# Silu as one ScalarE operation between two table loads, in the delta-rule stage of a three-layer kernel

## What is computed

```
q = silu(_short_conv(x @ Wq.T, conv_q))        # the same for k and v, four taps
beta = jax.nn.sigmoid(x @ Wb.T)
q, k = _l2norm(q), _l2norm(k)                  # per head
def step(S, inp):                              # a scan over the 512 tokens
    q_t, k_t, v_t, b_t = inp
    v_new = (v_t - einsum('bhd,bhdm->bhm', k_t, S)) * b_t[..., None]
    S = S + einsum('bhd,bhm->bhdm', k_t, v_new)
    return S, einsum('bhd,bhdm->bhm', q_t, S)
```

## Time and profile before

| | |
|---|---|
| median of 3 runs | 744.13 us (742.5 to 744.98) |
| profiled execution | 742.86 us, its span 741.1 us |
| granted TensorE clock, mean | 0.936 of full speed |
| busy: PE, DVE, ACT, POOL | 610.2, 596.0, 477.6, 471.5 us |
| steps begin on DVE at (us) | 52.4, 90.1, 134.5, 180.8, 227.2, 273.6, 319.6, 362.8 |

### The profile page before, as it was taken

The page is one execution under the profiler, slowest core; times in us unless marked ns, Lnnn a source line. Parts: engine busy times, 40 slices in busy tenths (PEclk is TensorE's granted clock), DMA queues, the critical chain, the costliest instruction groups (busy, mean ns, idle before and its releaser), DMA issues.

```text
span 741.1 us, 17464 instructions
## 1 busy us (share of the span) xinstructions
PE 610.2 (82%) x5443; PEld 490.8 (66%) x5443; DVE 596.0 (80%) x1698; ACT 477.6 (64%) x1270; POOL 471.5 (64%) x494
## 2 busy tenths in 40 slices
PE   4826365897998979977687989989999999979797
PEld 3614143685876858766567658768887787957776
DVE  4499989899999999999988768888897888654435
ACT  3984748799797996967367647465574736563442
POOL 2017999699898998989928714425507723673534
PEclk9956666899999999999998989999999999999999
DMA  6331221303214031130020343345546645655722
GB/s 233 74 76 57 57 75 47 100 16 83 65 42 118 14 74 57 40 105 15 1 71 2 100 111 116 101 145 154 154 134 173 179 128 148 187 165 142 201 86 75
DMA packets 104687, 72.70 MB, mean 98 GB/s; under 512 B 44832, under 2 KB 92576, under 8 KB 104352
## 3 DMA queue, kind: packets, MB, share of 16 engines
q1 hardware_dynamic: 100000, 62.27, 29.6%
q0 software_dynamic: 4608, 9.45, 4.7%
HBM read 44.48 MB, written 27.20 MB: 97 GB/s over the span
## 4 chain that ended last, share of the span: by engine, by line
PE 25%; ACT 7%; DVE 6%; SPq 4%; issue 4%; DMA 4%; POOL 1%; DVEq 0%; ACTq 0%; POOLq 0%
PE bank L2146 4%; PE bank L2127 4%; PE bank L2050 3%; PE bank L2019 3%; PE bank L2174 2%; PE bank L1882 2%; ACT prod_mem L1321 2%; PE bank L2117 1%; DMA hid<-in_w 1%; ACT wv L1363 1%; SPq L637 1%; POOL s_xs L966 1%; PE bank L2056 1%; SPq L640 1%; PE bank L1854 1%
## 5 line engine op out<-in xcount | busy, mean ns | idle before, releaser
L1854 PE MATMUL bank<-w,hid 128*128 128x128 f32 x768 | 100.5, 287 | 24.5 <-DVE y_even L2737 13.1
L1854 PEld LDWEIGHTS bank<-w,hid 128*128 128x128 f32 x768 | 95.5, 201 | 34.6 <-ACT hid L1189 10.8
L898 POOL TENSOR_TENSOR oq_mem<-hist_mem,q_t 128x384 f32<-128x384 f32 (+1 forms) x96 | 101.4, 1090 | 0.0
L1189 ACT ACTIVATE hid<-bank 128x512 f32<-128x512 f32 x112 | 62.4, 594 | 35.6 <-PE bank L1834 34.9
L2146 PE MATMUL bank<-w,wv 128*128 x428 | 61.1, 286 | 11.6 <-ACT wv L1363 10.9
L2146 PEld LDWEIGHTS bank<-w,wv 128*128 128x128 f32 x428 | 53.0, 194 | 18.5 <-issue 18.1
L2605 DVE TENSOR_REDUCE hist_mem<-hist_mem 128x64 f32<-128x320 f32 x128 | 62.3, 486 | 3.4
L981 POOL DMA_INDIRECT qkv<-s_ys,back_at x32 | 30.4, 952 | 52.5 <-DMA s_ys<-q_t 42.6
L1762 PE MATMUL bank<-xnT_h,wtap_h 128*128 128x512 f32 x104 | 49.7, 478 | 16.1 <-DVE qkv L2559 6.7
L1832 PE MATMUL bank<-xT_h,w_h 128*128 128x512 f32 x112 | 50.7, 453 | 11.7 <-ACT hid L1189 11.5
L2595 DVE TENSOR_REDUCE u<-prod_mem 128x32 f32<-128x288 f32 x128 | 57.6, 450 | 3.4
(11 more groups left out here) (302 smaller groups left out, 1745.4 us busy)
## 6 DMA issues: line engine op xcount, KB each, us to landing
hid<-in_w SPq DMA_DIRECT2D x72, 128.0 KB
s_qkv<-qkv SPq DMA_DIRECT2D x24, 256.0 KB, 2.6
pin<-s_xs SPq DMA_DIRECT2D x71, 64.0 KB
pin<-s_qkv SPq DMA_DIRECT2D x16, 256.0 KB, 2.9
kk<-in_w SPq DMA_DIRECT2D x30, 128.0 KB
s_ys<-q_p SPq DMA_DIRECT2D x28, 128.0 KB
s_ys<-q_t SPq DMA_DIRECT2D x23, 128.0 KB
s_xs<-zeros SPq DMA_DIRECT2D x40, 64.0 KB
```

The source lines that it names most:

```text
L898: tt(oq[:, :, j, :, 0:HD], s_at, bc(turned[:, n, j], 2, HD), ALU.mult).then_inc(o_part, 1)
L1189: nc.scalar.activation(hid[:, e % 2, f], bank[:, ZB + f, :], ACT.Relu).then_inc(hid_ready, 1)
L1854: last = nc.tensor.matmul(bank[:, y_bank(e, wide), tokens], hid[:, e % 2, f, tokens], w2[:, e, f], start=(f == 0), stop=(f == FC - 1))
```

## The change

ACT now applies Silu itself, from the bank into qkv, one operation for each of q, k and v; the three sigmoid operations and DVE's multiplication are gone. Silu is in another table set than Exp and Ln, so a load stands before and one behind each group: two in each of the steps 0 to 5 and six in the opening. `out_norm` (Ln, Exp) moves ahead of the first load, v's Silu and the second load ahead of `xf_rstd`. PE projects v ahead of `moe_down(n, 3)`, still behind `out_project`. `delta_kdot` on DVE moves from gap (5, 0) to (4, 2). In the opening, SP stores k of chunk 0 before it loads chunk 2's x, and loads it back before v.

```diff
             v_out(0, first=True)
             beta_out(0)
+            k_out(0)
             first_x(2)
+            beta_in(0)
+            k_in(0)
             v_in(0)
-            beta_in(0)
-            k_out(0)
-            k_in(0)
             q_out(0)
...
-            def prep_sigmoid(c, z):
-                src = bank[:, (QB, KB, QB)[z], :]
+            def prep_silu(c, z):
                 act.wait_ge(projected, 4 * c + z + 1)
-                nc.scalar.activation(sig[:, z], src, ACT.Exp, scale=-1.0).then_inc(sig_exp, 1)
-                act.wait_ge(sig_exp, 3 * c + z + 1)
-                nc.scalar.activation(sig[:, z], sig[:, z], ACT.Ln, bias=one_col[:]).then_inc(sig_log, 1)
-                act.wait_ge(sig_log, 3 * c + z + 1)
-                nc.scalar.activation(sig[:, z], sig[:, z], ACT.Exp, scale=-1.0).then_inc(sig_ready, 1)
+                if due(16 * c):
+                    act.wait_ge((q_stored, k_stored, v_stored)[z], 16 * c)
+                nc.scalar.activation(qkv[:, z], bank[:, (QB, KB, QB)[z], :], ACT.Silu).then_inc(silu_ready, 1)
...
                 if out:
                     out_square(o)
-                if prep:
-                    prep_sigmoid(c, 0)
-                if out:
                     out_norm(o)
                 if prep:
-                    prep_sigmoid(c, 1)
+                    nc.scalar.preload_act_table_set("silu_and_others")
+                    prep_silu(c, 0)
+                    prep_silu(c, 1)
                 delta_turn(i)
                 if out:
                     xf_centre(o)
                 if moe:
                     moe_scale(n, 3, wide=False)
                     moe_expert(n, 4)
+                if prep:
+                    prep_silu(c, 2)
+                    nc.scalar.preload_act_table_set("natural_log_exp_and_others")
                 if out:
                     xf_rstd(o)
                 if moe:
                     moe_expert(n, 5)
                 if out:
                     xf_scale(o)
-                if prep:
-                    prep_sigmoid(c, 2)
...
             w1_round()
-            first_sigmoid(0, 2)
-            first_sigmoid(1, 0)
+            nc.scalar.preload_act_table_set("silu_and_others")
+            first_silu(0, 2)
             first_square(0, 0)
+            first_silu(1, 0)
+            nc.scalar.preload_act_table_set("natural_log_exp_and_others")
             xn_centre(2)
             first_norm(0, 0)
-            first_sigmoid(1, 1)
-            first_sigmoid(1, 2)
+            nc.scalar.preload_act_table_set("silu_and_others")
+            first_silu(1, 1)
+            first_silu(1, 2)
             first_square(1, 0)
             first_square(1, 1)
+            nc.scalar.preload_act_table_set("natural_log_exp_and_others")
             first_beta(1)
...
                 if out:
                     out_project(o)
+                if prep:
+                    prep_project(c, 2)
                 if moe:
                     moe_down(n, 3, wide=False)
                     moe_up(n, 4)
-                if prep:
-                    prep_project(c, 2)
-                if moe:
                     moe_up(n, 5)
...
-                elif at == (5, 0):
+                elif at == (4, 2):
                     if ahead:
                         delta_kdot(i + 1)
...
-                elif at == (6, 3):
-                    if prep:
-                        prep_silu(c, 0)
```

More of the change, by code:

```diff
@@ L1383, in taps_round, with first_silu @@
                 nc.scalar.copy(wtap_h[:, TAPS[g]], wtap[:, TAPS[g]]).then_inc(taps_high, 1)
-            def first_sigmoid(c, r):
+            def first_silu(c, r):
                 z, name = ((1, "k"), (2, "v"), (0, "q"))[r]
@@ L1389, in first_sigmoid @@
                 if c:
[L1390 to L1395, removed]
+                    act.wait_ge((k_stored, v_stored, q_stored)[r], 16)
+                nc.scalar.activation(qkv[:, z], bank[:, FIRST_BANKS[c][name], :], ACT.Silu).then_inc(silu_ready, 1)
             def first_beta(c):
@@ L1433, in _ @@
             first_rstd(1)
+            nc.scalar.preload_act_table_set("silu_and_others")
             taps_round(1)
             taps_round(2)
-            first_sigmoid(0, 0)
-            first_sigmoid(0, 1)
+            first_silu(0, 0)
             first_square(0, 1)
+            first_silu(0, 1)
+            nc.scalar.preload_act_table_set("natural_log_exp_and_others")
             first_beta(0)
@@ L2553, in prep_xnT_rest @@
                    xnT_h[:, :, KC - 1:].bitcast(F32), ALU.subtract).then_inc(xnT_rest, 1)
[L2555 to L2559, removed]
             def prep_qk(c):
@@ L2790, in taps_rest @@
                 tt(wtap_l[:, TAPS[g]], wtap[:, TAPS[g]], wtap_h[:, TAPS[g]].bitcast(F32), ALU.subtract).then_inc(taps_low, 1)
[L2792 to L2798, removed]
             def first_k(c):
@@ L2874, in between @@
                     delta_qdot(i)
-                elif at == (10, 0):
-                    if prep:
-                        prep_silu(c, 1)
                 elif at == (10, 3):
@@ L2880, in between @@
                         moe_mix(n, 4)
-                elif at == (12, 0):
-                    if prep:
-                        prep_silu(c, 2)
                 elif at == (13, 0):
@@ L2940, in _ @@
             taps_scale(2)
-            first_silu(0, 0)
             taps_rest(2)
             prep_xnT_rest(1, tb=TB)
-            first_silu(0, 1)
             first_k(0)
-            first_silu(0, 2)
             w1_rest()
@@ L2949, in _ @@
             out_weights()
-            first_silu(1, 0)
             first_q(0)
-            first_silu(1, 1)
             delta_kdot(0)
-            first_silu(1, 2)
             first_solve()
```

## The result

The changed kernel takes 748.01 us (median of 20 runs), the kernel before 742.73 (20 runs): a ratio of the means of 1.0051, 95% interval 1.0031 to 1.0071, so **slower by 2.3 to 5.3 us**, 3.8 in the middle (the two medians stand 5.3 apart). The forecast of +1.4 us had the sign and was too small; 748.01 lies in the range (737.5 to 750), and the outcome in the case that had 0.33.

What follows compares the result with a forecast made beforehand. Steps 2 to 5 were taken to last as long as ACT's list plus ACT's and PE's waits for each other. -0.95 - 0.5 - 0.95 + 3.8 = +1.4 us on 742.86: 744.3 (745.5 in the median's terms), range 737.5 to 750.

Steps and rivals of the forecast that it cites:

- the case that had 0.33: Whole kernel: the outcome slower, beyond the about 0.3% (2.2 us) that a measurement can tell; chance 0.33.
- opening: Before the steps: q's norm unmoved, later Silu and squares earlier, DVE's first product at 52.0 for 52.96; -0.95 us.
- step 0: First step, no experts: DVE gains 1.4 us but waits some 0.9 more for POOL's kk; net -0.5 us.
- step 1: Second step, no experts: q's saving vanishes in DVE's wait for out_project, k's and v's stay; -0.95 us.
- steps 2 to 5, each: Full steps with experts: ACT falls behind at expert 3 and waits 0.2 us more later; about 0.95 us longer each.
- What bounds the kernel: Steps 2 to 5: ACT's list plus ACT-PE mutual waits set the length; DVE has at least 0.8 us slack.
- the walkthrough: Step 4 followed on ACT and PE: expert 3's y_odd at 252.3 for 251.56, delta_stage some 0.75 us later.
- ACT's price of a load: On ACT: a table load takes 1.4 us, its 1.28 plus the 0.1 it can't overlap.
- DVE the bound: All six steps: DVE sets their length, each gains 1.4 us; -9.4 in all, 734.8 us; chance 0.08.
- PE's move harmless: Steps 2 to 5: ACT makes its 0.7 us good later, 0.2 each; -1.6 in all, 742.5 us; chance 0.12.
- a load nearly free: Opening and steps 2 to 5: loads run beside ACT's waits; -6.1 in all, 738.0 us; chance 0.10.
- rival 2: Opening and steps 2 to 5: each counted load costs 1.28 us more; +10.3 in all, 754.4 us; chance 0.12.

Runs made afterwards that it cites:

- after_again: The changed kernel timed once more, unedited: 748.55 us, ratio 1.0057 to the kernel before.
- mults_back: The changed kernel plus three multiplications of constants on DVE in the gaps where silu's stood: 920.43 us, ratio 1.0156 to the kernel before.
- before_load: The kernel before plus one load of the table set already there, ahead of xf_rstd in steps 0 to 5: 750.88 us against 742.92, ratio 1.0094.
- no_loads: The changed kernel without the 12 loads of the steps, with Relu for Silu there: 910.4 us, ratio 1.0029 to the kernel before.
- after: The changed kernel as first timed and profiled, against the kernel before: 748.01 us, ratio 1.0051.
- sp_only: The kernel before with only SP's new order in the opening: 742.21 us, ratio 0.9985 to the kernel before.

## Why the prediction was off, step by step

Against the sum of +1.4 us, by the steps:

| term | predicted | measured |
|---|---|---|
| opening | -0.95 | about 0 |
| step 0 | -0.5 | -1.1 to -1.4 |
| step 1 | -0.95 | -0.8 and -1.4 at a like clock |
| steps 2 to 5, each | +0.95 | +1.35 |
| step 6 | nothing | +0.2 and +0.6 |
| whole | +1.4 | +2.3 to +5.3 |

In after_again these add up to +4.0 us at step 7 (366.7 against 362.8), as the whole does (+3.8). Why step 6, which has no load, got longer was not followed.

**What bounds the kernel** was right: DVE's busy time fell by 8.4 us in the steps 0 to 6 (289.7 to 281.3) and bought nothing in the full steps; mults_back put three multiplications a step back and lost nothing there. The forecast of 12 us (18 x 0.68) had the row's duration where its own 0.46 each gives 8.3. DVE's wait for xT_h grew to 2.0 us a step, where the walkthrough had some 3: another 1.6 us a step went to the wait for PE at an even expert.

**ACT's price of a load** (1.4 us) was right: 1.4 in before_load, 1.4 in no_loads. The two Silu behind the first load take 0.97 us of ACT's list (248.67 to 249.64), 0.49 each, for the 0.54 taken. That the first load is hidden and the second counts was right, by no_loads.

**The steps 2 to 5** were mis-sized, and this is the term that failed: +0.95 where 1.35 was measured, 1.6 us over four steps. The path was right, its last part was left out. The failing sentence is "ACT waits 0.2 us more. From there ACT's list is as before." The 0.22 is there, but PE itself is late by then. Relu 5 stands 2.6 us later than before, relative to the step (v's Silu and the load now stand ahead of it), so PE waits 1.17 us for it where it went straight on before; `moe_up(7)` is late, and ACT waits 0.16 us for it at xT_h and loses the overlaps beside both waits. I had followed ACT's list to the end of the step, and PE's only to expert 5. It was in reach: in the trace of before PE goes from `moe_down(3)` at 247.36 to the end of `moe_down(5)` without a pause, and has only 0.56 us of wait ahead of `moe_up(7)` to give.

**The opening** was wrong by 0.95. Eight traces with this opening have the first product at 51.6 to 53.5 us, mean 52.5; three with the old list of ACT have 51.96, 51.99 and 52.96. Against a scatter of 1 us or more a single run settles nothing, but the gain isn't there in the mean. Two steps of the account can be named from the rows of after. First, q's norm ended at 37.8, not at 37.1, and the Silu of chunk 1's q ran at 41.2, not 40.5: 0.7 us of the 0.95. The first of the added loads was not in my account; in after and after_again the second cast of the taps stands behind it at 13.0 (12.0 in before), in the six other traces at 12.1 to 12.2, so it is not the whole of the 0.7. Second, the first product no longer follows at once the copy that DVE awaits. After, and then before:

```profile
52.23 0.36 ACT L1092 COPY bank<-pin 128x256 f32<-128x256 f32 x1
53.11 0.42 DVE L2579 TENSOR_TENSOR prod_mem<-hist_mem,bank 128x256 f32<-128x256 f32 x1 [2.01 <-ACT prod_mem L1093]
```

```profile
52.51 0.36 ACT L1092 COPY bank<-pin 128x256 f32<-128x256 f32 x1
52.96 0.42 DVE L2587 TENSOR_TENSOR prod_mem<-hist_mem,bank 128x256 f32<-128x256 f32 x1 [0.46 <-ACT bank L1092]
```

It began 0.10 us after the copy's end in the three traces with the old list, and 0.52 to 0.54 in all ten with the new one, where DVE had stood idle for 2.0 us and not for 0.5. The code of both kernels waits for the same two staging operations there, L1090 and L1092 (the view names the next one, L1093, since the product began behind its end). Why, no run here shows.

**Step 0** gained 1.4 in after, not 0.5, and 0.4 of this is the same delay counted from its other side: the step is measured from the first product, which came late, while ACT and POOL went on. k of chunk 1 was issued for loading 0.43 us behind the end of ACT's second copy of the keys in before, in after and in sp_only alike, so it did hang on ACT's staging, as the prediction had it. The rest is a wait that did not grow: I had DVE wait 0.9 us more for POOL's kk, and it waited 0.22 as before (0.16). Opening and step 0 together ended 0.7 to 1.2 us earlier in after_again and after than in before (89.4 and 88.9 against 90.1), where -1.45 was forecast.

**The rivals.** 1 (DVE the bound) and 4 (PE's move harmless; it costs 0.6) are refuted. 3 (a load nearly free) is refuted where the load stood, and is what v_early makes true for the second one. 2, the load that costs twice its row, is refuted: nothing stands behind a load but 0.01 us. The Trainium skill, page "ScalarE: Activation LUTs", section "What ACT_TABLE_LOAD costs", gives 1283 ns for the load, as here (1.28 us), and about 1380 ns more for a DRAIN; the trace does not agree with the second, since an explicit load between two operations costs 1.4 us in all.

That the change was slower is thus no matter of the load's price, for which rival 2 had its chance, but of its place. The range held the result with some luck: the steps 2 to 5 and the opening were forecast too short, step 0 too long.

## What to carry to other kernels

Where engines wait for each other in a ring, an instruction costs what it pushes, so put it into a wait that the trace shows: the same load of 1.28 us, with v's Silu, made the step 1.3 us longer behind Relu 4 than ahead of the y_odd that was awaited. Follow a delay on **every** engine of the ring to the end of the step, not on the one that you changed. And before believing one profiled execution, compare it step by step, with the clock of each stretch beside it: here a part without any edit differed by 6 us, of which 3.5 lay in one stretch at a lower clock.

## Not expected

- TensorE's granted clock moves the end of this kernel by more than the change does. The profiled execution of after was 5.8 us below its own median, and with a clock of 0.57 or 0.79 over k's projection step 1 took 44.6 or 42.9 us.
- A DVE multiplication of the same 128x512 with both operands in SBUF took 0.74 to 1.77 us beside a busy POOL, from a bank 0.68. The Trainium skill, page "SBUF — State Buffer", section "SBUF: two separate sides", says that a DVE operation with two SBUF inputs and a GpSimd operation that reads SBUF hold a pair of ports in turn, the later one blocked. The spread agrees with that; no run here separates it, and these multiplications also read a small block over and over, which silu's did not. The longer rows also mean that mults_back overstates what the removed multiplications cost.
